# ScalarE's decay factors taken in another order, in a gated delta-rule layer with routed experts

## What is computed

```python
h = silu(conv(rms_norm(x)))                       # causal, 4 taps
q, k = unit(h @ wq), unit(h @ wk)                 # 8 heads of 64
v = h @ wv                                        # 8 heads of 128
sd, ab, bb = h @ w_spike, silu(h @ w_au + b_au) @ w_ad + b_ad, h @ w_beta + b_beta
for t in range(256):                              # per sequence and head
    mem = 0.9 * mem + sd[t]
    spike = mem > 0.5;  mem = mem - 0.5 * spike
    alpha = sigmoid(ab[t] + alpha_spike * spike)  # decay, 64 values per head; 1 if no spike
    beta = sigmoid(bb[t] + sum(spike * beta_spike)) * any(spike)
    s = s * alpha
    s = s + beta * outer(k[t], v[t] - k[t] @ s)   # state, 64 x 128
    y[t] = q[t] @ s
x = layer_norm(x + x + (head_norm(y) @ w_out) * gate(x) + ffn(...))
x = layer_norm(x + x + expert(x))                 # routed feed-forward
```

## Time and profile before

| | us |
|---|---|
| median of 3 runs | 2067.58 |
| lowest and highest of them | 2063.93, 2072.63 |
| profiled execution, its own time | 2079.9 |
| span of its instructions | 2078.1 |
| TensorE busy with matmuls | 1457.7 (70%) |
| VectorE busy | 1279.4 (62%) |
| ScalarE busy | 596.6 (29%) |
| GpSimd busy | 348.5 (17%) |

### The profile page before, as it was taken

How to read it: one execution, slowest core, us unless ns; L and a number is a source line. 1 busy time by engine, 2 the same in 40 slices (tenths; PEclk the granted TensorE clock), 3 DMA queues, 4 the chain that set the end, 5 groups by cost and what they waited for, 6 DMA issues and landing times. The chain is left out here.

```text
span 2078.1 us, 46460 instructions
## 1 busy us (share of the span) xinstructions
PE 1457.7 (70%) x18280; PEld 903.1 (43%) x18280; DVE 1279.4 (62%) x3385; ACT 596.6 (29%) x1212; POOL 348.5 (17%) x505
## 2 busy tenths in 40 slices
PE   1246886788778877797779776977797779566551
PEld 0113463256334643464336433653365336345541
DVE  1737766865577647865786478557965675343335
ACT  1132124322521243123413341324223412212221
POOL 2120031003200140014101410140013101100005
PEclk9577998899779988999799879987998789769995
DMA  2161000000010001000100010001000100302112
GB/s 72 72 253 22 19 10 7 21 19 21 2 26 19 10 13 27 16 12 13 27 16 12 12 27 16 12 13 27 11 17 12 23 16 12 103 17 76 33 30 81
DMA packets 110570, 64.74 MB, mean 31 GB/s; under 512 B 79873, under 2 KB 91329, under 8 KB 110354
## 3 DMA queue, kind: packets, MB, share of 16 engines
q1 hardware_dynamic: 99186, 38.52, 7.1%
q10 hardware_dynamic: 8448, 16.78, 2.2%
q0 software_dynamic: 2720, 6.36, 1.0%
HBM read 27.39 MB, written 34.24 MB: 30 GB/s over the span
## 5 line engine op out<-in xcount | busy, mean ns | idle before, releaser
L775 POOL COPY kx<-kend_t 32x256 f32<-32x256 f32 x256 | 113.1, 442 | 859.6 <-PE ps L1274 843.3
L1655 DVE SCALAR_TENSOR_TENSOR state<-state,gam,ps 128x128 f32<-128x128 f32 x512 | 137.5, 341 | 74.3 <-PE ps L1274 74.3
L1211 PE MATMUL ps<-wv,ident 128*128 128x512 f32 x320 | 169.1, 661 | 9.2 <-DVEq L1590 9.2
L1607 DVE TENSOR_TENSOR nv<-ps,nrm 128x512 f32<-128x512 f32 x64 | 44.2, 691 | 182.1 <-PE ps L1146 181.6
L1467 DVE TENSOR_TENSOR kq_leaf<-kq,eleaf 128x1024 f32<-128x1024 f32 x32 | 39.7, 1239 | 161.4 <-ACT dleaf L892 114.5
L1274 PE MATMUL ps<-w,kx 128*64 128x128 f32 x2048 | 132.5, 285 | 0.0
L1579 DVE TENSOR_TENSOR tmp<-kq,kq_blk 128x31 f32<-128x31 f32 (+15 forms) x248 | 115.2, 464 | 12.7 <-ACT mem L827 6.7
L1274 PEld LDWEIGHTS ps<-w,kx 128*64 128x64 f32 x2048 | 116.9, 143 | 13.6 <-issue 13.6
L1069 PE MATMUL ps<-yt,headind 128*16 128x512 f32 x128 | 87.1, 819 | 38.6 <-ACT yt L865 28.6
L1211 PEld LDWEIGHTS ps<-wv,ident 128*128 128x128 f32 x320 | 64.9, 213 | 90.4 <-issue 74.5
L1107 PE MATMUL ps<-kq_pair 64*32 64x32 f32 x2048 | 60.3, 220 | 61.5 <-DVE ab L1514 56.5
(11 more groups left out here) (317 smaller groups left out, 3188.3 us busy)
## 6 DMA issues: line engine op xcount, KB each, us to landing
slot_d<-zeros ACTq DMA_DIRECT2D x16, 1024.0 KB, 13.1
a_d<-kq_pair SPq DMA_DIRECT2D x8, 512.0 KB, 2.6
kq_blk<-a_d SPq DMA_DIRECT2D x32, 128.0 KB, 3.6
u_d<-kq SPq DMA_DIRECT2D x8, 512.0 KB, 2.6
ub<-u_d SPq DMA_DIRECT2D x128, 32.0 KB, 2.0
wall<-in_w SPq DMA_DIRECT2D x8, 512.0 KB, 8.0
xin<-slot_d SPq DMA_DIRECT2D x39, 64.0 KB, 1.8
made_d<-ye SPq DMA_DIRECT2D x39, 64.0 KB, 1.5
```

Source lines behind the costliest of these rows:

```text
L775: m = pool.tensor_copy(kx[part, :, b4, :], kend_t[part, g, 2 * q:2 * q + 2, :])
L1211: pe.matmul(bw.t[:, :], ident[:, :], wv[:, 0:512], start=True, stop=True)
L1655: k = dve.scalar_tensor_tensor(out=state[:, hp, b, :], in0=state[:, hp, b, :], scalar=gam[:, hp, b:b + 1], in1=bd[j].t[:, DV * x:DV * x + ...
```

## The change

On ScalarE, `factors(c, 1)` moves from behind `squares(c, 1)` to just behind `keys(c, 0)`, ahead of `turned(last, 3)`. `factors(c, 2)` moves from ahead of the copy of pair 1's end keys to behind the copy of pair 0's, which is ahead of `square_x(nxt)`, `keys(c, 2)` and `squares(c, 2)`. `factors(c, 3)` moves in the same way, to behind pair 1's copy, ahead of `rsqrt_x(nxt)`, `keys(c, 3)` and `squares(c, 3)`. Nothing is added or taken away, and the other engines keep their order.

```diff
         def body(c, nxt, last):
             factors(c, 0)
             keys(c, 0)
+            factors(c, 1)
             if last:
                 turned(last, NG - 1)
             squares(c, 0)
@@
                 if p + 1 < HP:
                     keys(c, p + 1)
                     squares(c, p + 1)
-                    factors(c, p + 1)
                 b = bank_of[f"kend{p}"]
@@
                 act.activation(kend_t[:, :, p, :], b.t[:, :].rearrange("p (g k) -> p g k", g=NG),
                                ACT.Copy).then_inc(b.drained.sem, 1)
+                if p + 2 < HP:
+                    factors(c, p + 2)
                 if nxt and p == 0:
                     square_x(nxt)
                 if nxt and p == 1:
```

## The result

| | before | after |
|---|---|---|
| median, us | 2067.58 | 2111.22 |
| lowest and highest, us | 2063.93, 2072.63 | 2103.12, 2116.01 |
| span of the profiled execution, us | 2078.1 | 2114.2 |

The changed kernel is slower by a ratio of 1.0205 (95% interval 1.0166 to 1.0245). The forecast was 2124 us, with a range of 2098 to 2143, so the size was some 13 us too high. Run once more later, beside other kernels, the ratio was 1.0226 (1.0173 to 1.0279).

The account below looks back on a forecast made before the run. Bound: a chain across engines in the pair stage, not the exponentials alone. Queues 36.4 us, last chunk 2.2, TensorE's clock 14 and 3.9 sum to 56.5 us, on a median of 2067.6: 2124 us, range 2098 to 2143.

Parts of the forecast that it names:

- What bounds the kernel: Pair stage: a chain across engines, with pair 1's exponentials only the last 3.45 us of VectorE's 11.69 us wait.
- The rival in which the exponentials leave the chain with nothing in their place: Pairs 1 and 2 each start 3.45 us earlier in 8 chunks, gain up to 55 us: 2012; chance 0.04.
- First move: Pair 1's exponentials ahead of the turned tile: copies and TensorE's work behind move by 3.45 us, pair 1 gains 0.2.
- The term for the clock: TensorE's turned tile and squares of pair 0, fifth chunk alone: high clock lost behind a longer pause, +3.9 us.
- Second move: Pair 2's exponentials ahead of the next chunk's square: TensorE's mean square and keys 6.9 us later, pair 2 +3.3 us.
- the clock ahead of the mean square: TensorE's pause grows from 1.38 to 4.8 us; low clock makes mean square and pair 2's keys 2.0 us longer.
- The rival in which the clock holds: TensorE's clock stays high behind the longer pause, queues alone cost 38.6 us: 2106; chance 0.20.
- the 14 us: Low clock at TensorE's mean square and pair 2's keys over the whole kernel: 7 x 2.0 us.
- Third move: Pair 3's exponentials ahead of the root: the convolution waits about 1.9 us and starts 5.2 us later than before.
- Last chunk: Without a next chunk's square and root, the exponentials still go ahead of the keys: +2.2 us, bounds 0 and 3.45.
- Worse: Rival: clock stays low through pair 1's products and pair 2's squares too, some 19 us more: 2143; chance 0.10.
- no change: Rival: TensorE's unexplained 1.59 us pause shrinks and VectorE's slack helps, some 5 us a chunk won back: 2071; chance 0.06.

Follow-up runs that it names:

- e1: Kernel before with only pair 1's exponentials moved, ahead of the turned tile, those of pairs 2 and 3 at their old places; ratio 1.0112 to the kernel before.
- e5: Kernel before with the exponentials of pairs 1, 2 and 3 moved directly behind the squares of pairs 0, 1 and 2; ratio 0.9911 to the kernel before.
- e7: As e5, but pair 1's exponentials behind the turned tile's second copy and ahead of its output copy; ratio 0.9882 to the kernel before.
- e8: The changed kernel itself, measured and traced a second time; ratio 1.0226 to the kernel before.
- e2: Kernel before with only the exponentials of pairs 2 and 3 moved, ahead of the next chunk's square and root; ratio 1.0107 to the kernel before.
- e4: Changed kernel with four idle matmuls in TensorE's pause ahead of the next chunk's mean square; ratio 1.0198 to the kernel before.
- e3: Changed kernel with the next chunk's square and root put ahead of the exponentials of pairs 2 and 3; ratio 1.0010 to the kernel before.

## Why the prediction was right, point by point

- **What bounds the kernel.** Right. The wait for L892 was only the last link of a chain through the turned tile, the squares, the keys and the leaf products. With the link gone, VectorE idled for TensorE instead: 11.63 us for 11.69 in e1, and 9.62 in the changed kernel, where the squares of pair 0 were faster by the clock. The rival in which the exponentials leave the chain with nothing in their place is excluded by the result, for the reason given, the missing idle time ahead of L872. e5 and e7 show that it comes true in part (18 and 24 us) as soon as the block stands where ScalarE idles.
- **First move.** The queues were right: L872 moved by a block, and pair 1 gained nothing by its early factors. TensorE's pause ahead of its second turn went from 2.38 to 4.52 us in the sixth chunk and not to the 5.8 forecast: the second turn came 3.3 us later, but the first one too had ended 1.2 us later, counted from pair 0's first product. The term for the clock was mis-sized and in part had the wrong sign. I had +3.9 us, for the fifth chunk alone; there it was +2.0, from 13.54 to 15.55. But in chunks 3, 4, 6 and 7 pair 1 came 2.0 to 2.3 us earlier, since the squares of pair 0, which took 3.57 us at the low clock, took 1.88 at the high one. All told -6.4 us in seven chunks. Nothing in the forecast led to a faster clock there. e1 has the same first move and the gain in one of these four chunks only, so it is not the move's own; it was there in all looped chunks of e8 too.
- **Second move and the clock ahead of the mean square.** Right, in mechanism and size. The pause was 4.67 us (forecast 4.8), with L798 as its releaser. The six instructions took 5.45 us in the sixth chunk instead of 2.81: 2.6 us, where I had taken 2.0 and a bound of 2.5. Pair 2 came 1.5 us behind its keys (forecast 1.3). From pair 1 to pair 2 it was 5.6 us more in the mean of seven chunks, against 3.3 + 0.2 + 2.0 = 5.5. That the two agree so closely is in part luck: chunk by chunk it was 3.5 to 8.1, and 4.8 in the mean in e8's trace. The rival in which the clock holds is excluded by the 0.50 in the row above, and by the mean square's 2.05 us in each of the looped chunks of the changed kernel, e2 and e8. (Behind a pause of 1.38 us the clock is not always high, though, as I had taken from the sixth chunk: see the last section.) As a cost of the whole kernel, the 14 us are not shown: e4 gave the place its high clock back, 12 us there, and lost as much elsewhere, a part at the low clock and a part in pauses for which the trace names no releaser.
- **Third move.** The wait of the convolution came, released by L805, at 1.36 us instead of 1.9. The term was mis-sized because I carried over 5.65 us from the keys of pair 2 to the copy of pair 1's end keys, which was 5.38 after the change (1240.16 - 1234.78), and because pair 2 itself started 0.2 us later behind its keys. This is 8.5 us in seven chunks for 13.
- **Last chunk.** +0.9 us for 2.2.
- **The sum.** 40.7 us in the pair stage, 36.1 in the span, 43.6 in the medians, for 56.5. The difference is the clock at pair 0's squares (10 us between +3.9 and -6.4) and the convolution (5 us); the other terms were off by 1 to 2 us each and nearly cancel.
- **Worse, or no change.** The clock did not stay low through the products of pair 1, and TensorE's unexplained pause behind the cross products did not shrink: in the mean of chunks 2 to 7 it was 1.76 us after the change and 1.66 before.

## What to carry to other kernels

An instruction block that an engine waits for is not moved forward for free: look at the idle time of its own engine at the new place, and at what stands behind it there. If the next instruction has no idle time ahead of it and another engine idles for it, the block goes on the path in full (e1), unless something behind it gets shorter by the move (e3); where the engine itself waits, it costs next to nothing (e5, e7). And a wait in the profile names the link that ended last: work out when the second condition of the same wait is met, since the time between the two is all there is to win. Here the leaf products were done at 1188.4 and VectorE started at 1192.06, so 3.7 us could be won. By the queues the change moves the leaf products by 3.45 and leaves 0.2; e5 left them nearly in place and won 3.6 us a chunk between pair 0 and pair 1.

## What the runs showed of the hardware

The granted clock of TensorE at one place can repeat from chunk to chunk and still differ between kernels that have the same instructions in the chunk up to there. The distance from pair 0 to pair 1 was 15.4 to 15.6 us in chunks 2 to 8 of both traces of the changed kernel, with the squares of pair 0 in 1.88 us, and 17.6 to 17.9 in chunks 2 to 8 of e3, with the squares in 3.57. It need not repeat: the kernel before and e1 have both values, and at the squares of pair 1 the two traces of the changed kernel disagree. Behind TensorE's pause of 4.67 us the clock was low in all 18 looped chunks of the changed kernel, e2 and e8, with the mean square in 2.05 us. Behind the pause of 1.38 us it was high, with the mean square in 1.10, in 28 of the 30 looped chunks of the kernel before, e1, e3, e5 and e7. The fifth chunk of e1 and the third of the kernel before were low there:

```profile
551.73 2.04 PE L1007 MATMUL ps<-xsq,meanw 128*128 128x512 f32 x2 [1.38 <-ACT xsq L798]
```

So a short pause does not secure the high clock, though it is high there far more often. What decides where it falls stays open. A forecast of a few microseconds per chunk that hangs on it can miss even the sign, as the +3.9 us for pair 0's squares did.

Four matmuls more in the loop, in e4, went with pauses of 1 to 2 us on TensorE at places where it had none before, and with none where it had one. No releaser stands in the trace for them.
